# Four whole groups of gathered rows by SyncE, six rows a step, in place of two and a part

## What is computed

```python
h = relu(layernorm(x))
p1 = tanh(h @ pp_W1 + pp_b1) @ pp_W2 + pp_b2
inter = concat([p1[src], p1[dst]]) @ pi_W1 + pi_b1
inter = ((inter @ pi_W2 + pi_b2) @ pi_W3).reshape(E, 64, 8)
i1 = einsum('ecb,eb->ec', inter, edge_attr)
i1 = tanh(i1 @ ii_W1 + ii_b1) @ ii_W2 + ii_b2
out = x + segment_sum(i1, dst, N)
```

## Time and profile before

| | |
|---|---|
| median of three runs | 1986.8 us (1985.95 to 1989.17) |
| the profiled execution's own time | 1983.09 us |
| its span | 1981.2 us |
| busy: PE, DVE, ACT, POOL | 87%, 73%, 56%, 75% |
| mean granted TensorE clock | 0.963 |
| DMA queues, share of 16 engines: hardware, software | 17.9%, 15.4% |
| data moved | 127.83 MB, 65 GB/s |

### The profile page before, as it was taken

One profiled execution on the slowest core, in us unless ns is written; L12 is line 12 of the kernel. 1 busy time (PEld: TensorE's weight loads), 2 busy tenths in 40 slices (PEclk: granted clock), 3 DMA queues, 4 the chain that ended last, 5 costly groups with the idle time before them and its releaser, 6 DMA issues.

```text
span 1981.2 us, 58993 instructions
## 1 busy us (share of the span) xinstructions
PE 1733.1 (87%) x20012; PEld 1134.5 (57%) x20012; DVE 1449.0 (73%) x1939; ACT 1109.5 (56%) x2419; POOL 1479.1 (75%) x1569
## 2 busy tenths in 40 slices
PE   7699999989988898888888888888888888888998
PEld 6466566655555555555555555555555555555666
DVE  7688778877677777677777777677777767777766
ACT  5666656655555555555555555555555555555554
POOL 7777777777777777777777777777777777777773
PEclk9799999999899999999999999899999999999999
DMA  6543333333333332332333323333233233332331
GB/s 141 115 82 62 67 67 64 61 65 66 58 63 58 62 66 56 63 62 56 62 55 61 62 56 60 61 63 64 55 63 62 56 59 62 59 59 54 59 71 44
DMA packets 266170, 127.83 MB, mean 65 GB/s; under 512 B 188169, under 2 KB 238328, under 8 KB 265864
## 3 DMA queue, kind: packets, MB, share of 16 engines
q1 hardware_dynamic: 214767, 74.86, 17.9%
q0 software_dynamic: 49664, 50.96, 15.4%
q10 hardware_dynamic: 1558, 0.15, 0.1%
HBM read 119.42 MB, written 6.00 MB: 63 GB/s over the span
## 4 chain that ended last, share of the span: by engine, by line
POOL 62%; issue 21%; PE 11%; ACT 2%; DMA 1%; SPq 1%; DVE 1%; ACTq 0%; DVEq 0%; POOLq 0%
POOL u_rows L568 62%; PE bank L1379 5%; PE bank L1474 1%; PE bank L1362 1%; DMA loc_bc<-loc_tab 1%; PE bank L1386 1%; PE spread_ps L1371 1%; DVE o_sb L987 1%; PE bank L1346 1%; ACT st_sb L756 0%; SPq L472 0%; SPq L440 0%; PE spread_ps L1208 0%; PE bank L1356 0%; DMA v_tab<-acc_all 0%
## 5 line engine op out<-in xcount | busy, mean ns | idle before, releaser
L568 POOL DMA_INDIRECT u_rows<-u_tab,src_e x1424 | 1352.4, 950 | 434.1 <-issue 433.1
L987 DVE TENSOR_TENSOR o_sb<-st_sb,spread_ps 128x2048 f32<-128x2048 f32 x391 | 892.9, 2284 | 365.0 <-PE spread_ps L1371 346.8
L756 ACT ACTIVATE st_sb<-bank,s_bias 64x256 f32<-64x256 f32 x1564 | 734.3, 469 | 438.0 <-PE bank L1362 406.9
L1379 PE MATMUL bank<-o_sb,g_sb 128*64 128x256 f32 x6256 | 807.0, 403 | 1.0 <-DVE o_sb L987 0.8
L1379 PEld LDWEIGHTS bank<-o_sb,g_sb 128*64 128x64 f32 x6256 | 433.5, 143 | 232.9 <-issue 36.7
L1362 PE MATMUL bank<-ident,u_rows 128*128 128x128 f32 x1436 | 259.3, 304 | 191.9 <-DMA u_rows<-u_tab,src_e 191.0
L1051 DVE TENSOR_TENSOR hot_t<-loc_bc,bank 126x512 bf16<-126x512 bf16 x391 | 268.8, 688 | 144.0 <-PE bank L1474 59.7
L1362 PEld LDWEIGHTS bank<-ident,u_rows 128*128 128x128 f32 x1436 | 189.8, 192 | 240.5 <-DMA u_rows<-u_tab,src_e 228.0
L1474 PEld LDWEIGHTS bank<-hot,t_sb 128*65 128x65 f32 x3128 | 216.1, 139 | 158.6 <-issue 150.6
L744 ACT ACTIVATE tt_sb<-bank,z_bias 128x256 f32<-128x256 f32 x391 | 185.4, 474 | 175.1 <-PE bank L1379 174.4
L1474 PE MATMUL bank<-hot,t_sb 128*65 128x42 f32 x3128 | 262.8, 235 | 9.1 <-DVE acc_all L1100 8.6
(11 more groups left out here) (148 smaller groups left out, 353.3 us busy)
## 6 DMA issues: line engine op xcount, KB each, us to landing
loc_bc<-loc_tab SPq DMA_DIRECT2D x391, 126.0 KB
u_rows<-u_tab,src_e POOLq DMA_INDIRECT x1424
sp_stage<-u_tab SPq DMA_DIRECT2D x1344, 0.2 KB
v_win<-v_tab SPq DMA_DIRECT2D x391, 15.8 KB
basis<-edge_attr SPq DMA_DIRECT2D x24, 256.0 KB, 4.2
v_tab<-acc_all SPq DMA_DIRECT2D x6, 336.0 KB
basis<-u_tab,src_e POOLq DMA_INDIRECT x100, 2.7
u_tab<-basis SPq DMA_DIRECT2D x6, 224.0 KB
```

Of the source, the lines that this page charges most:

```text
L568: pool.indirect_dma_start(out=u_rows[:, g % UR, j, :] if g >= AHEAD else first_u[:, g - XG, j, :], out_offset=None, in_=u_tab[:, :], in_of ...
L756: last = nc.scalar.activation(tiles[h * D:(h + 1) * D, j], s_ps[part].rearrange("p (q a e) -> p q a e", q=2, a=TILES), ACT.Identity, bias= ...
L987: return nc.vector.tensor_tensor(o_sb[:, r, :, :].rearrange("p c (j e) -> p j c e", j=TILES), st_sb[:, r, :].rearrange("p (j e) -> p j e", ...
L1379: last = nc.tensor.matmul(z_ps[h * D:(h + 1) * D, 0:2 * P], g_sb[:, c, :], o_sb[:, r, c, 2 * h * P:(2 * h + 2) * P], start=(c == 0), stop= ...
```

## The change

The groups that SP brings are now 96, 183, 270 and 357, from steps 4, 91, 178 and 265 on, six rows a step, so that a group takes 86 steps; the last group is POOL's, which waits for `last_in` before it. `sp_idx` holds a group's 512 indices in one partition, and they are read into registers eight at a time. One DMA places a group. In all 2048 rows. v's window is loaded in the order of the table, so that part w of node n lies in partition 3n+w; `iota_p` becomes p divided by 3, made by integer operations (p*171 shifted right by 9). The window starts are read without the runtime check.

```diff
-    BY_SP = [(135, 4, P), (263, 132, P), (NG - 1, 260, PART)]
+    ROWS = 6
+    BY_SP = [(96, 4), (183, 91), (270, 178), (357, 265)]
+    AT_ONCE = 8
...
-        sp_idx = sb("sp_idx", [P, len(BY_SP) * TILES], i32)
+        sp_idx = sb("sp_idx", [1, len(BY_SP) * GE], i32)
...
-            def fetch_rows(k, p):
-
-                _, at = nc.values_load_multi_w_load_instructions(
-                    sp_idx[p:p + 1, k * TILES:(k + 1) * TILES], engines=[mybir.EngineType.SP], min_val=0, max_val=N - 1,
-                    skip_runtime_bounds_check_because="src names nodes of x")
-                for j in range(TILES):
-                    sp.dma_start(sp_stage[p:p + 1, k % 2, j, :], u_tab[bass.ds(at[j], 1), :]
+            def fetch_rows(k, rows, at):
+
+                for r in rows:
+                    p, j = divmod(r, TILES)
+                    if r % AT_ONCE == 0:
+                        _, at = nc.values_load_multi_w_load_instructions(
+                            sp_idx[0:1, k * GE + r:k * GE + r + AT_ONCE], engines=[mybir.EngineType.SP], min_val=0,
+                            max_val=N - 1, skip_runtime_bounds_check_because="src names nodes of x")
+                    sp.dma_start(sp_stage[p:p + 1, k % 2, j, :], u_tab[bass.ds(at[r % AT_ONCE], 1), :]
                                  ).then_inc(sp_rows_in[k], 16)
+                return at
...
-                sp.wait_ge(sp_rows_in[k], 16 * TILES * n)
-                for j in range(TILES):
-                    sp.dma_start(u_rows[:, g % UR, j, :], sp_stage[:, k % 2, j, :]).then_inc(fetched[k], 16)
+                g, _ = BY_SP[k]
+                sp.wait_ge(sp_rows_in[k], 16 * GE)
+                sp.dma_start(u_rows[:, g % UR, :, :], sp_stage[:, k % 2, :, :]).then_inc(fetched[k], 16)
...
                         _, starts = nc.values_load_multi_w_load_instructions(
-                            base_row[0:1, g:min(g + 8, NG)], engines=[mybir.EngineType.SP], min_val=0, max_val=N - W)
+                            base_row[0:1, g:min(g + 8, NG)], engines=[mybir.EngineType.SP], min_val=0, max_val=N - W,
+                            skip_runtime_bounds_check_because="VectorE made them from dst and cut them at N - W")
...
-                    sp.dma_start(v_win[:, g % VR, :], v_tab[bass.ds(start, W), :, :].rearrange("n w d -> w n d")
+                    sp.dma_start(v_win[:, g % VR, :], v_tab[bass.ds(start, W), :, :].rearrange("n w d -> (n w) d")
...
-                        if 0 <= g - first_at < n:
-                            fetch_rows(k, g - first_at)
+                        if first_at <= g:
+                            at = fetch_rows(k, range(ROWS * (g - first_at), min(ROWS * (g - first_at + 1), GE)), at)
...
                 for g in range(XG, NG):
                     k = g // PIECE
+                    if g == FULL:
+                        pool.wait_ge(last_in, 32)
...
-            nc.vector.tensor_copy(iota_p[:, 0:1], iota_i[:, 0:1])
             nc.vector.tensor_scalar(iota_i[:, 1:2], iota_i[:, 0:1], NB - 1, None, ALU.bitwise_and)
+            nc.vector.tensor_scalar(iota_i[:, 2:3], iota_i[:, 0:1], 171, None, ALU.mult)
             dve.drain()
-            for k in (1, 2):
-                nc.vector.tensor_scalar(iota_p[:, k:k + 1], iota_p[:, 0:1], float(k * W), float(W), ALU.is_ge,
-                                        ALU.mult)
+            nc.vector.tensor_scalar(iota_i[:, 0:1], iota_i[:, 2:3], 9, None, ALU.logical_shift_right)
...
-            nc.vector.tensor_tensor(iota_p[:, 1:2], iota_p[:, 1:2], iota_p[:, 2:3], ALU.add)
+            nc.vector.tensor_copy(iota_p[:], iota_i[:, 0:1])
...
-            nc.vector.tensor_tensor(iota_p[:, 0:1], iota_p[:, 0:1], iota_p[:, 1:2], ALU.subtract)
...
-                            pe.wait_ge(fetched[skipped.index(n + u)], 16 * TILES)
+                            pe.wait_ge(fetched[skipped.index(n + u)], 16)
...
-                for of in skipped[:-1]:
+                for of in [of for of in skipped if of < LOOP_END]:
```

More of the change, by code:

```diff
@@ L107, in program @@
         iota_f = sb("iota_f", [P, BW])
-        iota_i = sb("iota_i", [P, 2], i32)
-        iota_p = sb("iota_p", [P, 3])
+        iota_i = sb("iota_i", [P, 3], i32)
+        iota_p = sb("iota_p", [P, 1])
         iota_8 = sb("iota_8", [P, 1])
@@ L428, in load_sp_idx @@
             def load_sp_idx():
-                for k, (g, _, n) in enumerate(BY_SP):
-                    sp.dma_start(sp_idx[0:n, k * TILES:(k + 1) * TILES],
-                                 src[g * GE:g * GE + n * TILES].rearrange("(p j) -> p j", j=TILES)
+                for k, (g, _) in enumerate(BY_SP):
+                    sp.dma_start(sp_idx[0:1, k * GE:(k + 1) * GE], row(src[g * GE:(g + 1) * GE])
                                  ).then_inc(sp_idx_in, 16)
-            def fetch_rows(k, p):
-                _, at = nc.values_load_multi_w_load_instructions(
-                    sp_idx[p:p + 1, k * TILES:(k + 1) * TILES], engines=[mybir.EngineType.SP], min_val=0, max_val=N - 1,
-                    skip_runtime_bounds_check_because="src names nodes of x")
-                for j in range(TILES):
-                    sp.dma_start(sp_stage[p:p + 1, k % 2, j, :], u_tab[bass.ds(at[j], 1), :]
+            def fetch_rows(k, rows, at):
[6 more added lines that the diff above has]
+                    sp.dma_start(sp_stage[p:p + 1, k % 2, j, :], u_tab[bass.ds(at[r % AT_ONCE], 1), :]
                                  ).then_inc(sp_rows_in[k], 16)
+                return at
             def place_fetched(k):
-                g, _, n = BY_SP[k]
-                sp.wait_ge(sp_rows_in[k], 16 * TILES * n)
-                for j in range(TILES):
-                    sp.dma_start(u_rows[:, g % UR, j, :], sp_stage[:, k % 2, j, :]).then_inc(fetched[k], 16)
+                g, _ = BY_SP[k]
+                sp.wait_ge(sp_rows_in[k], 16 * GE)
+                sp.dma_start(u_rows[:, g % UR, :, :], sp_stage[:, k % 2, :, :]).then_inc(fetched[k], 16)
             def store_early(lo, hi):
@@ L469, in _ @@
                 load_sp_idx()
+                at = None
                 for g in range(NG):
@@ L492, in _ @@
                         sp.wait_ge(sp_idx_in, 16 * len(BY_SP))
-                    for k, (of, first_at, n) in enumerate(BY_SP):
+                    for k, (of, first_at) in enumerate(BY_SP):
                         if k >= 2 and g == first_at:
                             sp.wait_ge(s_ready, BY_SP[k - 2][0] + 1)
-                        if 0 <= g - first_at < n:
-                            fetch_rows(k, g - first_at)
+                        if first_at <= g:
+                            at = fetch_rows(k, range(ROWS * (g - first_at), min(ROWS * (g - first_at + 1), GE)), at)
                         if g == of - 3:
@@ L560, in _ @@
                     k = g // PIECE
+                    if g == FULL:
+                        pool.wait_ge(last_in, 32)
                     if g % PIECE == 0:
                         pool.wait_ge(ld[k % LD], ld_count(k))
-                    if g in [of for of, _, _ in BY_SP]:
+                    if g in [of for of, _ in BY_SP]:
                         continue
@@ L1409, in y_late @@
                     last.then_inc(y_ps, 1)
-            skipped = [of for of, _, _ in BY_SP]
+            skipped = [of for of, _ in BY_SP]
             def step(n, u, first, last_pass, g=None, fetched_pass=False, gone=(0,) * UN):
@@ L1504, in _ @@
                     at += UN
-                with pe.Fori(at, LOOP_END, UN) as n:
-                    for u in range(UN):
-                        step(n, u, False, False, gone=gone)
+                if at < LOOP_END:
+                    with pe.Fori(at, LOOP_END, UN) as n:
+                        for u in range(UN):
+                            step(n, u, False, False, gone=gone)
                 for n in range(LOOP_END, NG + 5, UN):
@@ L1510, in _ @@
                         step(n, u, False, True, fetched_pass=True, gone=gone)
+                        if n + u in skipped:
+                            gone[u] += 1
                 pe.wait_ge(acc_done, NG)
```

## The result

| | before | changed |
|---|---|---|
| median, lowest and highest run (us) | 1986.97 (1985.95 to 1989.17, 4 runs) | 1973.22 (1969.94 to 1977.05, 4 runs) |
| profiled execution, its span (us) | 1983.1, 1981.2 | 1969.9, 1968.1 |
| first and last gather of POOL start at | 42.4, 1954.5 | 40.9, 1948.2 |
| behind the last gather, to the end of the span | 26.7 | 19.9 |

The ratio is 0.993, with a 95% interval of 0.9909 to 0.9951. So two things need an answer: why the forecast's 8 was too small, and what the other 3 us are.

The account below looks back on a forecast made before the run. The prediction took POOL, a conveyor of indirect DMA gathers waiting for nobody, to bound the kernel. Its terms -10.0 + 2 + 0 = -8 us, off the median 1986.8, gave 1978.8 us, range 1974.5 to 1988.

Parts of the forecast that it names:

- Part 1: POOL's gathers ahead of the end: four skipped groups before group 382 instead of two, -10.0 us.
- Part 2: POOL's gathers while SP fetches rows: more small transfers lengthen some of POOL's instructions, +2 us, bounds 0 to 3.9.
- Part 3: SP's pace at the start: eight steps +0.4 us, 1.5 us late by step 33, within 3.4 us slack, term 0.
- Part 4: Everything else, such as iota arithmetic, v rows' order, one placing issue a group and PE's unrolled pass: nothing.
- The end: After POOL's group 382: a landing, eight more groups at PE's own pace, and 15.8 us of tail.
- rival C: At the end, group 382's late landing and halved clock do not come back: -10.5 us, 1976.3 us; chance 13%.
- The range: The whole kernel's predicted time, with some rivals and 1 us of run scatter: 1974.5 to 1988 us.
- A's stall: At the start's buffer ring, v's issue stays 0.75 us, POOL stalls 7.6 us, gain gone: 1986.8 us; chance 14%.
- Rival B: At the same ring, SP's rows get dearer waiting for queue room: +7.5 us, 1994.3 us; chance 7%.

Follow-up runs that it names:

- r2: The kernel before, run again unaltered for a second profile: 1982.85 us against 1982.04, ratio 1.0001.
- e5: The kernel before with only v's row order and its iota as in the change: 1984.97 us against 1984.45, ratio 1.0005.
- e6: The kernel before without the early stores of out, the rest stored at the end in one piece: 1981.88 us against 1982.04, ratio 0.9999.
- r1: The changed kernel, run again unaltered: 1972.42 us against 1983.04 for the kernel before, ratio 0.9941.
- e7: The changed kernel without the early stores of out, the rest stored at the end in one piece: 1972.17 us, ratio 0.9947 to the kernel before.
- e9: The changed kernel with the piece loads of src and edge_attr eight steps later: 1975.32 us against 1984.45 for the kernel before, ratio 0.9958.
- e2: The changed kernel with group 357 gathered by POOL, so SP brings three groups: 1977.37 us against 1983.04 for the kernel before, ratio 0.9975.
- e10: The kernel before with only groups 135 and 263 by SP, the last group gathered by POOL: 1986.05 us against 1984.45, ratio 1.0007.
- e4: The changed kernel with SP reading no row numbers and fetching no rows, zeros instead: 1973.7 us against 1982.04 for the kernel before, ratio 0.9961.
- e1: The changed kernel with v's window loaded part first, as before the change: 1983.13 us against 1983.04 for the kernel before, ratio 1.0001.
- e12: The kernel before with each fetched group placed by one DMA instead of four: 1979.5 us against 1980.34, ratio 0.9995.
- e3: The changed kernel with the runtime checks of the window starts back: 1977.27 us, ratio 0.9968 to the kernel before.
- e8: The changed kernel with five groups by SP, seven rows a step, numbers read sixteen at a time: 1974.3 us against 1984.45 for the kernel before, ratio 0.9948.
- e11: The changed kernel with five groups by SP, five rows in the first 36 steps, then seven or eight: 1967.03 us against 1980.34 for the kernel before, 0.993.

## Why the forecast was too small

The mean of four profiles of the kernel before, or of ones that stand to it at 0.9999 to 1.0005 (before, r2, e5, e6), beside that of four of the changed one (changed, r1, e7, e9) makes the sum. The first column is the time from the first gather to the last, the second from there to the end.

| | gathers | behind them | first gather |
|---|---|---|---|
| before-like | 1911.8 | 27.2 | 41.9 |
| changed-like | 1907.3 | 21.0 | 41.7 |
| difference, in all -10.9 | -4.5 | -6.2 | -0.2 |
| forecast, in all -8.0 | -5.0 + 2 | -5.0 | 0 |

So of the 2.9 us between forecast and profiles 1.5 are in the gathers, 1.2 behind them and 0.2 at the start. The other 2.8 of the first comparison's 13.7 are scatter between comparisons, above all the kernel before's high median there.

- **Part 1, right.** Of the forecast's -10.0, half is four gathers fewer, and half is that the last gather is group 390's instead of 389's, one group nearer to the end. e2 (5.0 us for a group) and e10 (group 390's worth nothing) show both halves, and that it is the number of groups skipped ahead of the place where the chain leaves POOL that counts. The prediction put that place at 382, as in its one profile; without a late landing it is 386. No group between them is skipped, so the term is the same.
- **Part 2, the step that failed first.** The +2, taken "in the middle, since the trace can't tell these apart" between 0 and 3.9, is +0.5 by the table, within the scatter of single profiles (1906.1 to 1908.7 in the changed kernel's four), and nothing by e4. The loss of 0.006 us a gather in the earlier trace rows (0.007 with 1092 distances, which makes the upper bound some 4.5) had been put down to the rows because a stretch of one profile without rows had none; e5's stretch without rows has it in full, and e4 has it with no rows at all. The mechanism was wrong, and with it the middle: its true size is the lower bound, 0.
- **Part 3, right.** v's issue was 0.32, not 0.42, which is 8 x 0.10 = 0.8 us in eight steps, and the sum came out 0.6 lower (35.0, not 35.6); SP was 3.6 us earlier at group 33 instead of 1.5 later. The bounds 0.32 to 0.75 held. e1 shows why this place was worth the working: with v's issue 0.43 us longer in each step, all of the gain is gone.
- **Part 4, right** as far as tried: the placing in one DMA brought 0.8 us with an interval that holds zero.
- **The end, mis-sized.** Forecast -5.0 behind the last gather, measured -6.2. Counted from group 386's last gather to the end of the span, the four profiles like before have 41.7, 43.5, 42.2 and 41.3 us, the four like the changed kernel 39.9, 43.1, 40.7 and 40.3; in e2, e10 and e12 it is 40.1, 40.1 and 40.3. From PE's matmuls of group 386 on all sixteen need 36.6 to 37.6. The 37.4 and 37.6 are e6's and e7's, which store more at the end; the others have 36.6 to 37.0. So some 40 us is the end without a late landing, what comes on top is up to 3.5, and the missing 1.2 is that it was 2.2 in the mean before and 1.0 after. With four profiles each, and ranges that overlap, this can be chance; the four placing DMAs ahead of group 385's rows (r2, e6), which the changed kernel no longer has, are the candidate that e12 did not settle. In the first comparison rival C came true in part. In that execution of the changed kernel the clock fell to 0.73 from 1900 to 1905, ahead of the stores at 1909.2, and not to 0.50 behind them, and PE was level with POOL again at 386. In r1 the landing and the clock did come back, at 1909 and 1915, and r1 still had 10.6 us. C was right that the stores delay the landing of group 382, and wrong that it costs what it said: e6 and e7 without the stores gained nothing in the median. It also named group 390 as what sets the end then; it is 386.
- **The range, too tight at its low end.** C's 1976.3 less one microsecond for scatter is 1975.3, and the prediction doesn't say how it comes to 1974.5. The median of the kernel before alone stood 2.5 to 6.6 us higher in the first comparison than in the later ones (1987.0 against 1980.3 to 1984.5), which the three runs shown, within 3.2 us of each other, could not tell. Against the -10.6 of r1 and the -9.9 of e7, the forecast of -8 is off by 2 to 3 us.

Rivals A and B did not come true here, but e1, e3 and e8 made A's stall on purpose, and found it where it was placed. It hung on one figure, v's issue, as the prediction had it. Rival B did not decide: one row's instruction (L443) took up to 1.262 us, its median is 0.228. The rule of the Trainium skill that stood beside it (Perfetto Trace Analysis, "DMA Optimizations": batch transfers under 2 KB) names a cost that SP does pay, 0.42 us for each 256 B, and e8, which pays it for seven rows a step, stalls; the 704 more transfers of this change found room for it.

## What to carry to other kernels

When one engine is a conveyor, count the pieces that it need not carry ahead of the place where it stops to set the pace; pieces behind that place are worth nothing. Then find the one stretch in which the helper's queue, not the conveyor, has no slack (here the start of the ring of eight buffers, from 205 to 260 us), and pay for every added transfer there with cheaper ones, or bring fewer there and more later, as e11 does. An optimisation of the helper's queue may measure as nothing alone and be worth all of the gain in company, so a test in the old kernel says little on it.

## What was not expected of the hardware

- Instructions of POOL over 1 us come in pairs 20 us apart, every 80 us, 0.1 to 0.6 us each above the median of 0.944, with rows in flight or without (e4: 610.38 1.53 us, 630.93 1.09 us). Many sit at the same few gathers of the program (32 of 42 in the changed kernel, 16 of 37 in e9). They are what the earlier trace rows showed one of. No run names the cause.
- The median gather was 0.947 us in two programs (e8, e10) and 0.944 or 0.945 in the others, a difference that goes with 4.1 us over the kernel in e10. Two variants that differ only there can't be told apart by a few tenths of a per cent.
- SP loading register values from SBUF took 0.81 us for four, 0.78 for eight and 1.23 for sixteen, so eight at a time are cheap, and sixteen still are by the value.
- The same bytes of v, issued with the slowest dimension of 3 took 0.75 us of SP's time, and as 126 runs 0.32.
- The late landing near the end and the low clock behind it move between executions of one program: group 382 and 0.50 in the first profile of the kernel before, group 385 and 0.55 in r2; 6.21 us and 0.50 in r1, no late landing on the chain and 0.73 in the first profile of the changed kernel. With them moves what lies behind the last gather: 19.9 us in one profile of it and 23.2 in the other.
